# An attention and quantised-FFN kernel: first three groups reordered, the FFN's down-projection turned, its casts spread over three engines

## The reference, cut to what matters

```python
x: (8, 256, 128)                                  # 16 heads of 64, one key and value head shared by all
xn = ln(x, g_norm)
q = l2norm(heads(xn @ Wq)) * q_scale
k, v = split(xn @ Wkv); k = l2norm(concat(null_k, k)) * k_scale; v = concat(null_v, v)
sim = einsum('bhid,bjd->bhij', q, k) * 8 + rel_pos_bias      # bias: a small MLP over distances, 255 + null
attn = softmax(where(causal & mask, sim, -max))
y = ln(reshape(attn @ v) @ Wout, g_out)           # (8, 256, 128) = 2048 tokens of 128
# the FFN, with fake quantisation by ONE scale over all of y and ONE scale over all of h
yq = round(y / sy) * sy                           # sy = sigmoid(clip) * max|y| / 127
h = silu(yq @ Wg.T) * (yq @ Wu.T)                 # 352 hidden columns
hq = round(h / sh) * sh                           # sh = sigmoid(clip) * max|h| / 127
out = x + hq @ Wd.T
```

## Time and profile before

| | us |
|---|---|
| median of 3 runs (lowest, highest) | 282.92 (282.5, 284.82) |
| the profiled execution | 284.12 |
| its span, from first to last instruction | 282.3 |
| what lies around the span | 1.8 |

### The profile page before, as it was taken

How to read it: one execution, slowest core, us unless ns; L and a number is a source line. 1 busy time by engine, 2 the same in 40 slices (tenths; PEclk the granted TensorE clock), 3 DMA queues, 4 the chain that set the end, 5 groups by cost and what they waited for, 6 DMA issues and landing times.

```text
span 282.3 us, 7419 instructions
## 1 busy us (share of the span) xinstructions
PE 258.2 (91%) x2210; PEld 209.5 (74%) x2210; DVE 234.2 (83%) x973; ACT 225.4 (80%) x778; POOL 201.4 (71%) x395
## 2 busy tenths in 40 slices
PE   6789899999999999999999999999999999988171
PEld 5457678888888888888888888888888877752060
DVE  5799797898889888988898889787977779879893
ACT  2587888988889898999899989998899898258380
POOL 6385878988798879888987888878878885013310
PEclk9999999999999999999999999999999999999757
DMA  5648000000000000000000000000000200000014
GB/s 136 182 117 188 1 2 1 2 3 0 3 0 5 0 3 0 2 1 3 0 2 3 2 0 2 1 3 2 0 2 2 78 2 1 2 4 2 1 34 119
DMA packets 12110, 6.48 MB, mean 23 GB/s; under 512 B 1615, under 2 KB 11940, under 8 KB 12069
## 3 DMA queue, kind: packets, MB, share of 16 engines
q1 hardware_dynamic: 11642, 5.78, 7.7%
q10 hardware_dynamic: 426, 0.20, 0.2%
HBM read 4.88 MB, written 1.07 MB: 21 GB/s over the span
## 4 chain that ended last, share of the span: by engine, by line
PE 79%; DVE 10%; ACT 4%; issue 3%; POOL 1%; DMA 1%; DVEq 0%; ACTq 0%; POOLq 0%
PE bank L976 16%; PE bank L927 11%; PE front L953 9%; PE back L1019 7%; PE front L1019 7%; PE bank L790 7%; PE back L953 6%; PE bank L808 5%; DVE score L1376 2%; ACT bias L749 2%; PE front L766 1%; PE bank L934 1%; ACT prob L744 1%; DVE prob L1543 1%; PE bank L906 1%
## 5 line engine op out<-in xcount | busy, mean ns | idle before, releaser
L633 ACT ACTIVATE prob<-score,negmax 128x258 f32<-128x258 f32 (+1 forms) x256 | 113.7, 451 | 17.5 <-DVE negmax L1376 17.4
L491 POOL TENSOR_SCALAR prob<-prob,rrow 128x258 f32<-128x258 f32 x254 | 105.8, 436 | 19.4 <-DVE rrow L1384 16.0
L450 POOL TENSOR_TENSOR rq<-qn,neghalf 128x8 f32<-128x8 f32 x32 | 53.7, 1679 | 2.7
L633 ACT ACTIVATION_READ_ACCUMULATOR prob<-score,negmax 128x1 f32 x256 | 49.3, 192 | 0.0
L976 PE MATMUL bank<-pT,val 128*64 128x256 f32 x496 | 47.9, 335 | 0.0
L976 PEld LDWEIGHTS bank<-pT,val 128*64 128x64 f32 x496 | 30.3, 136 | 15.2 <-issue 4.9
L1376 DVE CUSTOM_DVE_ANT_0 score<-front,bias 128x258 f32<-128x258 f32 (+1 forms) x128 | 38.0, 354 | 2.0 <-PE front L953 1.8
L1376 DVE CUSTOM_DVE_ANT_0 score<-back,bias 128x258 f32<-128x258 f32 (+1 forms) x128 | 37.4, 349 | 0.0
L927 PE MATMUL bank<-wout,oT 128*128 128x128 f32 x256 | 36.8, 288 | 0.4 <-DVE oT L1366 0.4
L1366 DVE COPY oT<-bank 128x512 f32<-128x512 f32 x32 | 22.1, 689 | 16.1 <-PE bank L976 15.9
L927 PEld LDWEIGHTS bank<-wout,oT 128*128 128x128 f32 x256 | 30.9, 191 | 4.4 <-DVE oT L1366 0.8
(11 more groups left out here) (228 smaller groups left out, 469.9 us busy)
## 6 DMA issues: line engine op xcount, KB each, us to landing
bias<-relative_table SPq DMA_DIRECT2D x8, 256.0 KB, 5.1
X<-in_x_dram SPq DMA_DIRECT2D x1, 896.0 KB, 5.4
out_dram<-prob SPq DMA_DIRECT2D x3, 256.0 KB, 2.5
prob<-in_L_cond_Wq_dram SPq DMA_DIRECT2D x1, 512.0 KB, 3.8
wout<-in_L_cond_Wout_dram SPq DMA_DIRECT2D x1, 512.0 KB, 5.3
prob<-in_L_ffn_w_down_dram SPq DMA_DIRECT2D x1, 176.0 KB, 2.4
X<-in_x_dram SPq DMA_DIRECT2D x1, 128.0 KB, 2.1
prob<-in_L_ffn_w_gate_dram SPq DMA_DIRECT2D x1, 128.0 KB, 2.2
```

The lines of the kernel that those rows point to most:

```text
L450: pool.tensor_tensor(dst, src, neghalf[:, 0:width], ALU.pow).then_inc(done, 1)
L491: pool.tensor_scalar(prob[:, par, h, cols], prob[:, par, h, cols], rrow[:, par, h, t:t + 1], 1.0, ALU.mult, ALU.mult).then_inc(normed, 1)
L633: act.activation(prob[:, par, h, cols], score[:, h % 4, cols], ACT.Exp, scale=-1.0, bias=negmax[:, par, h, t:t + 1], accum_out=rowsum[:, p ...
```

## The change

Four things are changed, and nothing of what is computed.

**Ahead of group 0.** On VectorE the first `split_low` moves forward to just ahead of `mlp_stats(1)` and `mask_tail` to just behind it; ScalarE's mask row is cut in two halves, the first far forward; `qT_make(0)` on TensorE stands ahead of the K transposes, `qT_evac(0)` ahead of `q_norm2(2)`, and the two aggregations of `x_stats(1)` behind `qT_evac(1)`. The first bias load is split in two of two heads each (ten transfers in place of eight).

**Groups 0 to 2.** VectorE follows an order written out by hand (`opening_group`). In group 0 both score pairs run back to back; `xT_evac(1)` on ScalarE moves from between group 0's exponentials to group 1, behind four of them. `x_stats(2)` moves from group 1 to the end of group 2, `x_normalise(2)` from group 2 into group 3 between the score pairs, `x_power(2)` on GpSimd behind `normalise` of group 2, `k_power(1)` and `q_power(4)` behind that of group 1; `x_stats(3)` moves to group 3. On TensorE the turns of groups 1 and 2 stand ahead of `q_make`, and the fillers between group 0's score pairs go.

**FFN up to the maximum.** Tile (2, 1) goes from `MADE` to `POOLED` (6 and 5 now), with three buffers in place of two. The two casts of `yq` that ScalarE made go to VectorE (chunk 3) and GpSimd (chunk 2). Behind the tiles TensorE gets 25 fillers in five parcels, each behind an `h_absmax`, and fillers up to the first cast.

**FFN behind the maximum.** Of the 11 casts to bf16 ScalarE keeps 8, VectorE takes (2, 2) and (3, 0), GpSimd (3, 1). Chunk 0 is made as before. Chunks 1 to 3 are made turned (down weights as the stationary operand, 512 tokens moving: 3 matmuls in place of 12, and 5 for chunk 3 in place of 20), ScalarE copies them out with the scale (`down_evac`), TensorE turns them back (12 transposes) and VectorE adds x straight out of PSUM. All five stores are issued by SP.

```diff
-POOLED = [(0, IT - 1), (1, IT - 1), (2, IT - 1), (LAST, 0)]
+POOLED = [(0, IT - 1), (1, IT - 1), (2, 1), (2, IT - 1), (LAST, 0)]
+CAST_POOL = [(LAST, 1)]
+CAST_DVE = [(2, IT - 1), (LAST, 0)]
...
-            for k in range(4):
+            for h, count, loaded in ((0, 2, ld_bias[0]), (2, 2, ld_bias_pair), (4, 4, ld_bias[1]), (8, 4, ld_bias[2]),
+                                     (12, 4, ld_bias[3])):
                 for blk in range(2):
...
-            for k in range(3):
+            for k in (1, 0, 2):
                 sp.wait_ge(res_ready[k], 1)
...   GpSimd, group(s)
-                if s.at == 2:
-                    x_power(2)
+                if s.at == 1:
+                    normalise(heads(1)[0:2])
+                    k_power(1)
+                    q_power(4, 0)
+                    return
...
                 normalise(heads(s.at)[0:2])
+                if s.at == 2:
+                    x_power(2)
...   GpSimd, FFN
+            x_cast(2, 4)
             for n, (k, f) in enumerate(POOLED):
...
+            for k, f in CAST_POOL:
+                pool.wait_ge(h8, ORDER[k, f] + 1)
+                pool.tensor_copy(hqb[:, f, 512 * k:512 * k + 512], hq[:, f, 512 * k:512 * k + 512]).then_inc(hq_pool, 1)
...   ScalarE, group(s)
+                if s.at == 1:
+                    xT_evac(1, halves(misc))
                 exponent(heads(s.at)[0])
-                if s.at == 0:
-                    xT_evac(1, halves(misc))
                 exponent(heads(s.at)[1])
...   ScalarE, FFN
-            x_cast(LAST, 2)
...
+                act.activation(downT[:, k, cols], down_ps[k][:, cols], ACT.Copy, scale=sdc[:, 0:1]).then_inc(downT_ready, 1)
+            for k, f in CAST_ACT:
+                h_cast(k, f)
+            for k in range(1, LAST):
+                down_evac(k, None)
+            for half in range(2):
+                down_evac(LAST, half)
...   TensorE, FFN
+                for n in range(len(TILES) - 5, len(TILES)):
+                    pe.wait_ge(hmax_ready, n)
+                    keep_busy(5, bank[6])
                 over_partitions(1)
+                keep_busy(11, bank[6])
+                for n in range(2):
+                    pe.wait_ge(h8, n + 1)
+                    keep_busy(3, bank[6])
...
+                down_packed(0)
+                down_make(1)
+                down_packed(1)
+                down_make(2)
+                down_packed(2)
+                down_turn(1, 0, range(4))
...
+                product.then_inc(down_done, 1)
+                down_turn(2, 1, range(4))
+                for half in range(2):
+                    down_turn(LAST, 2 + half, range(2 * half, 2 * half + 2))
...   VectorE
+            def opening_group(s):
+                dve.wait_ge(ld_bias[s.g], 16 * 2)
+                score_pair(heads(s.at)[0:2])
+                if s.at == 0:
+                    dve.wait_ge(ld_bias_pair, 16 * 2)
+                    score_pair(heads(0)[2:4])
+                    invert(heads(0)[0:2])
+                    x_normalise(1)
+                if s.at == 1:
+                    invert(heads(0)[2:4])
+                    qT_evac(2, 2, 0)
+                    q_normalise(3, 3, q_ps0[3])
+                    xT_split_low(1, 1)
+                    score_pair(heads(1)[2:4])
+                    invert(heads(1)[0:2])
+                    qT_evac(3, 3, 0)
+                    k_norm2(1)
+                    q_norm2(4, 0)
+                if s.at == 2:
+                    oT_copy(0)
+                    invert(heads(1)[2:4])
+                    k_normalise(1)
+                    score_pair(heads(2)[2:4])
+                    q_normalise(4, 0, q_ps)
+                    invert(heads(2)[0:2])
+                    q_norm2(5, 1)
+                    qT_evac(4, 0, 1)
+                    x_stats(2)
+                    split_low(1)
...   VectorE, group(s) from group 3 on
                 score_pair(heads(s.at)[0:2])
...
+                if s.at == 3:
+                    x_normalise(2)
                 score_pair(heads(s.at)[2:4])
...   VectorE, FFN
-                if k < 2:
+                if n < 3:
                     dve.wait_ge(x8, n + 1)
                     dve.tensor_copy(xqb[:, cols], xq[:, cols]).then_inc(xq_ready, 1)
...
+            def residual(n, t0, t1, passed):
+                dve.wait_ge(down_turned, n + 1)
+                blocks = turned_ps[n][:, 0:(t1 - t0) * P].rearrange("p (j c) -> p j c", c=C)
+                dve.tensor_tensor(res[:, t0:t1, :], blocks, X[:, t0:t1, :], ALU.add).then_inc(passed, 1)
```

More of the change, by code:

```diff
@@ L684, in group @@
                     for t in range(2):
-                        act.activation(unull[0:2 * H, t, :], misc[0:2 * H, 0:C], ACT.Copy,
+                        act.activation(unull[0:2 * H, t, :], unull_ps, ACT.Copy,
                                        scale=sel[0:2 * H, t:t + 1]).then_inc(unull_ready, 1)
+                    pT_evac(0, 2)
+                    pT_evac(0, 3)
+                if s.at > 1:
+                    if s.made is not None:
+                        q_square(s.made, q_ps)
+                    for i in range(GH):
+                        pT_evac(s.turned, i)
+                    if s.kv is not None:
+                        kv_evac(s.kv, front_tails)
+                    if s.kT is not None:
+                        kT_evac(s.kT, front_tails)
+                    if s.xT is not None:
+                        xT_evac(s.xT, front_tails)
+                    if s.yT is not None:
+                        yT_evac(s.yT)
+                if s.null is not None:
+                    null_evac(s.null)
                 if s.first and s.g == 3:
@@ L905, in null_output @@
                 for k in range(HP):
[L906 removed]
+                    last = pe.matmul(unull_ps, vnull[:, k, :], wout[:, k, :], start=k == 0,
                                      stop=k == HP - 1)
@@ L1105, in group @@
                     y_null(s.prev)
+                if s.at < 3 and s.turned is not None:
+                    turn(s, 0)
+                    turn(s, 1)
+                if s.at == 1:
+                    qT_make(3)
                 if s.made is not None:
@@ L1434, in group @@
                 score_pair(heads(s.at)[0:2])
-                if s.turned is not None:
-                    invert(heads(s.turned)[2:4])
-                if s.kz is not None and s.first:
-                    k_normalise(s.kz)
-                if s.at == 0:
-                    x_normalise(1)
+                invert(heads(s.turned)[2:4])
+                if s.at == 3:
+                    x_normalise(2)
                 score_pair(heads(s.at)[2:4])
-                if s.at == 0:
-                    qT_evac(2, 2, 0)
-                    q_normalise(3, 3, q_ps0[3])
                 invert(heads(s.at)[0:2])
-                if s.at < 2:
-                    split_low(s.at)
                 if s.g == 1 and s.prev is not None:
@@ L1461, in group @@
                     k_norm2(s.kv)
-                if s.kz is not None and not s.first:
+                if s.kz is not None:
                     k_normalise(s.kz)
```

284 lines of the change are left out of this document (150 added, 134 removed).

## The result

The changed kernel takes 281.52 us (median of 10 runs, 281.33 to 281.77). The kernel before, run beside it 10 times, takes 284.14 (282.4 to 284.82). The ratio is 0.9917, with a 95% interval of 0.9896 to 0.9938: a gain of 0.8%, or 2.3 to 2.6 us, where 279.3 and 3.6 less were forecast. The profiled execution of the changed kernel took 281.33, its span is 279.5 (282.3 before).

What follows compares the result with a forecast made beforehand. TensorE bounds the even attention, so only the opening and FFN were priced: opening 1.2, tiles 0.3, scale 0.15, rest 2.35, lock -0.4 sum to 3.6, giving 280.5 profiled, 279.3 against the median; range 277.4 to 281.7.

Steps and rivals of the forecast that it cites:

- the last line of the sum: Whole kernel: the profiled execution's forecast 280.5 lowered to 279.3, because the old profiled execution lay 1.2 above the median 282.92.
- opening: Up to the values of group 2: they start at 45.35 in place of 46.55, 1.2 earlier; bounds 0 and 2.0.
- tiles: FFN up to the maximum: moving tile (2, 1) and two casts gains 0.3; bounds 0 and 0.7.
- scale: Between amax and the first quantisation: 1.53 shrinks by 0.15 with a running TensorE clock.
- quantisation to last addition: FFN behind the maximum: spread casts and turned matmuls end the additions 1.9 sooner, before 0.4 off for the lock.
- the lock: Casts behind the maximum: GpSimd and VectorE share a port; 0.4 loss, half of 0.85; in full 279.7, chance 0.08.
- last addition to the end: Final stores: 1.05 MB from 275.2 at some 280 GB/s, span ending at 279.5; gain 0.45.
- faster: Whole kernel: chance 0.64 of a gain beyond about 1%, built from shares of the forecast and several rivals.
- The last store lands no sooner from SP: Rival, final stores: landing takes 3.9 instead of 2.6, with a queue ahead; +1.1, 280.4; chance 0.08.
- rounding of zero: Group 3 of the opening: the new wait for x_power(2) loses half a microsecond, yet the 1.2 gain was kept.
- the slower rival: Groups 4 to 31: GpSimd's normalisations meet VectorE's operations, 0.12 more each; at 0.2 per group 284.9; chance 0.04.

Runs made afterwards that it cites:

- before with fillers: The kernel before with nothing but the 42 FFN fillers added: 282.15, ratio 0.9948.
- experiment 6: Changed kernel with the old path behind the maximum put back: 281.04; the second (last) kernel also has x_power(2) ahead of group 2's normalisations: 280.41.
- experiment 4: Changed kernel with its last store issued by ScalarE: 281.52; changed kernel with token chunk 0 not stored: 280.75.
- experiment 3: Changed kernel with x_power(2) issued ahead of the four normalisations of group 2 on GpSimd: 280.80, ratio 0.9898.
- experiment 5: Changed kernel with chunk 0 scaled behind chunk 1's quantisation, x added on GpSimd before its cast, and chunk 0 stored first: 282.55, ratio 0.9978.
- the opening alone: The opening's changes alone, with the FFN of before: 283.32, ratio 0.9992.
- after without fillers: Changed kernel without its 25, 11 and 6 FFN fillers: 282.06, ratio 0.9963.

## Why the prediction was right and wrong

The forecast of 279.3 missed the 281.52 by 2.2; the range of 277.4 to 281.7 holds it. That the time would be less was right, but with a gain of 0.8% it lies within 1% of before rather than beyond it. The 2.2 come from two steps: 1.2 from the last line of the sum, which went from 280.5 to 279.3, and 0.8 from the sum itself (the rest is the 0.2 between the profiled execution and the median). The sum term by term, against the profiled execution:

| term | forecast gain | measured |
|---|---|---|
| opening | 1.2 | 0.90 |
| tiles | 0.3 | 0.40 |
| scale | 0.15 | 0.16 |
| quantisation to last addition | 1.9, less 0.4 for the lock | 1.95 |
| last addition to the end | 0.45 | -0.61 |
| sum | 3.6 | 2.8 |

(The prediction's own shares for "faster" add up to 0.62, not 0.64; nothing hangs on it.)

**The step that failed most: from 280.5 to 279.3.** The sum gave 280.5 for the profiled execution, and then 1.2 were taken off, since that execution lay 1.2 above the median shown. That took the distance for scatter that the changed kernel would have as well. But the distance came mostly from the two levels of before, which are 1.76 apart: the profiled execution was of the lower-clock level, and the three runs were of both. The change takes the lower-clock level away, and the sum, made on rows of that level, had already counted the gain of it. So the 1.2 counted it twice. Measured: 281.33 profiled and 281.52 as median, no distance. The profile had the sign of it (0.50 from 265 to 275), beside runs from 282.5 to 284.82. The experiments with fillers show the size: 2.0 between before at a clock of 0.979 or less and before with fillers, and one level instead of two.

**The term that was mis-sized: the stores.** 3.85 from the last addition to the end were forecast, 4.91 were measured, and 4.90 to 5.00 in the other three profiles with these stores unchanged. The rate (some 280 GB/s) and the 0.9 from the first issue to data (273.09 to 273.9) were right. Not foreseen were the hole at 277.2 and the slow end behind it. Part of the price is the bundling itself: at this rate a megabyte that starts at 273.9 cannot be through before 277.6, and chunk 0's quarter is worth 0.8. The old order starts them under the additions (271.25 in the last kernel of experiment 6) and, at the full clock, needs 3.4 to 3.6 behind the last one. "The last store lands no sooner from SP" was the rival nearest to this, with +1.1; its price was met (1.06) and its reason in half: the landings are 2.7 to 3.5 and not 3.9, and the issuing engine changes nothing (experiment 4); the bytes ahead of the last store are what counts (0.8 for a quarter of them). The Trainium skill ("DMA: Bandwidth & Descriptors", section "Issuing engines are not separate DMA queues") says that another issuing engine saves only time on the sequencer; the runs agree, 281.52 against 281.52.

**Opening.** First scores at 21.19 (21.5 forecast), head 6 at 30.91 (31.2), `q_square` at 36.27 (36.35), values of group 1 at 37.76 (38.2): each step held, and a little more was gained up to here than forecast. Then the wait: `x_power` ended at 42.6, as forecast, and `xn` at 43.3; but TensorE was at its turns at 42.6 and not at 42.8, and lost 0.86 instead of half a microsecond. Values of group 2 came at 45.62 (45.35). The "rounding of zero" that was taken off for this wait was the mistake; experiment 3 gives 0.7 for it. What was gained there, 0.93, reached the FFN as 0.90, so the slower rival, groups 4 to 31 in another phase, did not come. (Its price of 0.12 per normalisation was a mean: of the eight in the opening of before, six took 0.37 to 0.48, and two, 1.04 and 0.80, lay under the two `split_low` of VectorE, which read two inputs from SBUF. The eight score operations beside them, which read one from PSUM, lengthened none.)

**Tiles and scale.** 0.40 and 0.16 for 0.3 and 0.15. VectorE waited 0.55 for a pooled tile and not at its last product (262.67), so GpSimd and not ScalarE held the last tiles.

**Behind the maximum.** 8.46 were measured; the prediction had 8.50 without the lock and 8.90 with it. VectorE's two casts took 0.75, 0.42 each, as alone (0.43). GpSimd's took 1.07, where the same cast took 0.61 alone (253.32): it was GpSimd that waited, 0.46, and it ended at 272.03, just ahead of the matmuls at 272.17. Who loses depends on who is there first: in experiment 5 VectorE came second and lost 1.0. So the wait was real, and the 0.4 was not due by a margin of 0.14. (By the Trainium skill's section cited in experiment 5, and if VectorE's second cast also went ahead, GpSimd's 0.61 would end at 271.56 + 0.61 = 272.17, an estimate; the trace has 272.03, which agrees about.)

**What the rewritten path is worth.** The prediction gave the compute gain behind the maximum, 1.9, to the turned matmuls and the spread casts. Of the measured 1.95, 1.07 are had from the fillers alone (10.41 to 9.34; only 0.4 if the opening alone's 9.76 is taken), and 0.88 from the rewriting at the full clock. Its tail is 1.47 longer than that of the old path at the same clock (4.91 against 3.44). Together it loses 0.45 to 0.6 from the quantisation to the end (12.78 to 12.93 against 13.37), and putting the old path back makes after 0.5 faster. At the lower clock the rewritten path wins 0.6 instead (14.09 against 14.66 and 14.71). So the gain of 2.6 against before at the lower clock is: fillers 2.0, opening 0.9, tiles 0.4, and some 0.5 to 0.7 lost behind the maximum.

**Open.** Why the last bytes are slow. Some 20 GB/s for 0.5 to 1.5 us end the kernels before, after, and those of experiment 4; they are missing in before with fillers and in both of experiment 6. The packets in the traces say what the slow end is: in after from 278.45 to 278.80 they take 7.2% of the time of the 16 DMA engines, so about one engine works on alone, and it must have fallen behind the others. A candidate is on record too. In each of these kernels a packet of 16 KB on an instruction queue holds an engine for 0.93 or 0.94 us (1.04 in before and the opening alone), 4 to 7 us ahead of the end. In after (275.26) it lies inside the dense stores; in before with fillers (275.38) and the last kernel (273.43) it lies in a pause between them. Before and the opening alone have a second one, at 279.15 and 278.90, ahead of their last bytes, and the last data of the opening alone starts as it ends, at 279.82. That fits, but it is argued and not shown: the trace doesn't tie a packet to its engine, no edit moved one, and the slow ends of experiment 4 (1.2 us and more) are longer than a delay of 0.93 accounts for. Nor was before profiled in a run at 0.987, so that its clock behind the maximum is full there is inferred from its 282.41 beside 282.15. And what separates the runs of after without fillers (281.6 and 282.7) is not known.

## What to carry to other kernels

Where the runs of a kernel spread over two levels, ask which one the profile shows, and don't shift a sum made on it to a median that mixes them. Around a barrier on which TensorE has nothing to do, try a few paced fillers alone before rewriting the work behind it: here seven lines gave as much as the new FFN, 282.15 against 282.45. When compute at the end is made shorter, price the stores anew: bytes that had been spread under the additions come all at once, and end later behind them (4.9 against 3.4 to 3.6 here). And where a stage and the one behind it move against each other from one profile to the next, compare their sum.

## What the hardware showed that was not expected

- Two levels of one kernel, 284.17 and 282.41, told apart by a mean clock of at most 0.979 or at least 0.981 (with two runs at 0.976 in between, 282.77 and 282.95). With the clock at 1.2 GHz behind the maximum 12 down matmuls took 1.46, at 2.4 GHz 0.84.
- A GpSimd cast from int8 to bf16, 128x512, took 0.61 alone and 1.07 beside two of VectorE's. A VectorE quantisation of 128x512 with one input took 0.48 alone and 1.49 under a GpSimd addition (experiment 5).
- Issuing two stores of 128 KB from SP took 2.29 in after (274.69), and one 0.51 in the kernels with the old order (274.84 in the last). The slow issue wasn't what set the end: 0.48 from ScalarE gave the same time.
